# Gather of a deformable convolution: coefficients multiplied from PSUM, group outputs in one bank

## The reference

```python
def _L3_conv_ref(data_im, weight, offset_w, mask_w):
    ...
        w00 = ((1 - ly) * (1 - lx))[:, :, None]
        w01 = ((1 - ly) * lx)[:, :, None]
        w10 = (ly * (1 - lx))[:, :, None]
        w11 = (ly * lx)[:, :, None]
        val = w00 * gather(y0i, x0i) + w01 * gather(y0i, x1i) + w10 * gather(y1i, x0i) + w11 * gather(y1i, x1i)
        val = val * msk
        return val.reshape(B, C * K, Ho, Wo)
    offset = _conv(data_im, offset_w)
    mask = jax.nn.sigmoid(_conv(data_im, mask_w))
    col = _deform_im2col(data_im, offset, mask)
    out = jnp.einsum('op,bphw->bohw', weight, col)
    return out
...
x = x + _L0_conv_ref(_gn(x), L0_conv_mean_table, L0_conv_std_table, L0_conv_weight, L0_conv_bias, 4, 5, 5, 6)
x = x + _L1_conv_ref(_gn(x), L1_conv_gn_weight, L1_conv_gn_bias, L1_conv_w1, L1_conv_b1, L1_conv_w2, L1_conv_b2)
x = x + _L2_conv_ref(_gn(x), L2_conv_ln_w, L2_conv_ln_b, L2_conv_W_in, L2_conv_conv_w, L2_conv_conv_b, L2_conv_W_xproj, L2_conv_W_dt, L2_conv_b_dt, L2_conv_A_log, L2_conv_D, L2_conv_W_out)
x = x + _L3_conv_ref(_gn(x), L3_conv_weight, L3_conv_offset_w, L3_conv_mask_w)
```

## Time and profile before

| | us |
|---|---|
| median of three runs | 1004.47 (1001.02 to 1005.22) |
| the profiled execution | 999.45 |
| its span, first to last instruction | 997.5 |
| VectorE busy | 837.4 (84%) |
| TensorE busy | 780.8 (78%) |
| GpSimd busy | 574.7 (58%) |
| ScalarE busy | 375.1 (38%) |

### The profile page before, as it was taken

How to read it: one execution, slowest core, us unless ns; L and a number is a source line. 1 busy time by engine, 2 the same in 40 slices (tenths; PEclk the granted TensorE clock), 3 DMA queues, 4 the chain that set the end, 5 groups by cost and what they waited for, 6 DMA issues and landing times.

```text
span 997.5 us, 8280 instructions
## 1 busy us (share of the span) xinstructions
PE 780.8 (78%) x2364; PEld 372.8 (37%) x2365; DVE 837.4 (84%) x1164; ACT 375.1 (38%) x535; POOL 574.7 (58%) x528
## 2 busy tenths in 40 slices
PE   3445878587778688778777887768389999999996
PEld 1122323132322134444343544414265444444443
DVE  3888853899999778689999999985989989989994
ACT  1120056854445135311111111101067777686640
POOL 0000000177674047777777777777777777777774
PEclk9666989789999798567777777777569999999998
DMA  5000018000000541111111112137343735444422
GB/s 124 0 0 1 0 32 170 5 0 1 0 1 0 106 104 48 47 51 50 50 52 50 50 50 53 50 97 186 105 138 90 206 113 148 135 126 114 124 66 53
DMA packets 32339, 69.82 MB, mean 70 GB/s; under 512 B 12368, under 2 KB 12624, under 8 KB 31184
## 3 DMA queue, kind: packets, MB, share of 16 engines
q1 hardware_dynamic: 16080, 35.27, 13.1%
q0 software_dynamic: 15360, 31.49, 12.2%
q10 hardware_dynamic: 864, 2.64, 1.2%
HBM read 54.94 MB, written 5.77 MB: 61 GB/s over the span
## 4 chain that ended last, share of the span: by engine, by line
POOL 48%; issue 17%; DVE 11%; PE 7%; ACT 1%; DMA 1%; POOLq 0%; ACTq 0%; SPq 0%; DVEq 0%
POOL got L788 47%; DVE scratch L1185 6%; DVE scratch L1192 3%; PE PS L1064 1%; PE PS L922 1%; DMA G<-XN 1%; PE PS L1285 1%; PE PS L923 1%; PE PS L931 1%; PE PS L1057 1%; PE PS L941 1%; PE PS L1049 1%; ACT scratch L1143 0%; PE PS L624 0%; DVE st L138 0%
## 5 line engine op out<-in xcount | busy, mean ns | idle before, releaser
L788 POOL DMA_INDIRECT got<-corner_table,idx_slot x405 | 401.7, 992 | 123.4 <-issue 123.4
L1049 PE MATMUL PS<-parts,selb 96*128 96x512 bf16 (+1 forms) x256 | 89.3, 450 | 78.4 <-DVE scratch L1111 41.0
L1064 PE MATMUL PS<-scratch,wt 128*128 128x512 f32 x256 | 149.9, 717 | 0.5 <-DVE scratch L1192 0.5
L1492 PE MATMUL PS<-scratch,UZ 128*128 128x512 f32 (+1 forms) x288 | 133.6, 613 | 2.9 <-DVE scratch L1477 2.9
L788 POOL DMA_INDIRECT got<-corner_table,idx_all x75 | 80.6, 1075 | 60.7 <-DVE prime L1359 38.1
L823 PE MATMUL PS<-ln_g,w 128*128 128x32 f32 x576 | 97.2, 334 | 0.0
L823 PEld LDWEIGHTS PS<-ln_g,w 128*128 128x128 f32 x576 | 94.5, 257 | 0.0
L829 ACT ACTIVATE G<-PS 128x32 f32 (+1 forms) x32 | 6.2, 195 | 221.4 <-PE PS L823 221.3
L1064 PEld LDWEIGHTS PS<-scratch,wt 128*128 128x128 f32 x256 | 59.9, 234 | 59.4 <-issue 50.1
L1161 POOL TENSOR_TENSOR scratch<-scratch 128x1024 f32<-128x1024 f32 x16 | 37.6, 2348 | 77.1 <-ACT scratch L1143 77.1
L1469 ACT ACTIVATE scratch<-UZ,knot 128x512 f32<-128x512 f32 (+1 forms) x128 | 81.6, 708 | 0.4
(11 more groups left out here) (344 smaller groups left out, 1345.4 us busy)
## 6 DMA issues: line engine op xcount, KB each, us to landing
UZ<-dense_rows SPq DMA_DIRECT2D x24, 512.0 KB, 4.1
got<-corner_table,idx_slot POOLq DMA_INDIRECT x405, 2.5
UZ<-dense_rows SPq DMA_DIRECT2D x96, 64.0 KB, 2.2
XN<-ln_g SPq DMA_DIRECT2D x6, 256.0 KB, 5.1
got<-corner_table,idx_all POOLq DMA_INDIRECT x75, 2.6
corner_table<-scratch SPq DMA_DIRECT2D x1, 1056.0 KB
corner_table<-XN SPq DMA_DIRECT2D x1, 1056.0 KB
X<-in_x SPq DMA_DIRECT2D x4, 256.0 KB, 4.8
```

Of the source, the lines that this page charges most:

```text
L788: pool.indirect_dma_start(got[:, slot, tap, :, :].rearrange("p k c -> p (k c)"), None, tables[b], bass.IndirectOffsetOnAxis(ap=index[:, ta ...
L1049: last = nc.tensor.matmul(PS[:, first + n, :], selb[:, which, j, :], parts[:, bass.ds(i * CHUNK + n * BANK, BANK)], start=True, stop=True)
L1064: last = nc.tensor.matmul(PS[:, 4 + n, :], wt[:, W_SUM:W_SUM + P], dBC[:, j % 2, n * BANK:(n + 1) * BANK], start=False, stop=(j == PAIRS - 1))
L1492: last = nc.tensor.matmul(PS[:, n % 4, :], steps[rows, j, :, :].rearrange("p b c -> p (b c)"), ramps[k][rows, j, :], start=(j == 0), stop= ...
```

## The change

VectorE copies the coefficients of each group into bank 7, whose room is cut by slot, a group ahead, and the multiply reads them from there. The first copy stands at the end of `prepare(0)`, each further one between the multiply and the first addition of the turn before. The outputs of groups and pairs, which had banks 6 and 7 in turn, now share bank 6, in two parts of it; TensorE waits for the readout of the group (the pair) just before.

```diff
+        def coef_bank(slot, n=TAPS):
+            return PS[:, 7, slot * 4 * TAPS:slot * 4 * TAPS + 4 * n]
+
+        def next_coef(G, slot, n=TAPS):
+            return nc.vector.tensor_copy(coef_bank(slot, n), coef[:, bass.ds(G, 1), 0:n, :].rearrange("p o t k -> p (o t k)"))
...
             tell(v, nc.vector.tensor_tensor(prodg[:, 0:n, :, :].rearrange("p t k c -> p (t k) c"),
                                             got[:, slot, 0:n, :, :].rearrange("p t k c -> p (t k) c"),
-                                            coef[:, bass.ds(G, 1), 0:n, :].rearrange("p o t k -> p (o t k)").unsqueeze(2).to_broadcast([P, n * 4, C]),
+                                            coef_bank(slot, n).unsqueeze(2).to_broadcast([P, n * 4, C]),
                                             ALU.mult), l3["prod_done"], G + (SLOTS + 1))
+            next_coef(G + 1, (slot + 1) % SLOTS)
...
         def group_psum(slot):
-            return PS[:, 6 + slot % 2, 0:32]
+            return PS[:, 6, 32 * (slot % 2):32 * (slot % 2) + 32]
...
             pe.wait_ge(l3["col_done"], G + 1)
-            pe.wait_ge(l3["o_read"], G + (1 if slot else 2))
+            pe.wait_ge(l3["o_read"], G + 2)
...
         def pair_psum(m):
-            return PS[:, 6 + m % 2, 0:2 * C]
+            return PS[:, 6, 2 * C * (m % 2):2 * C * (m % 2 + 1)]
...
-                                            coef[:, G, 0:n, :].rearrange("p t k -> p (t k)").unsqueeze(2).to_broadcast([P, n * 4, C]),
+                                            coef_bank(slot, n).unsqueeze(2).to_broadcast([P, n * 4, C]),
                                             ALU.mult), l3["prod_done"], G + (SLOTS + 1))
+            if G + 1 < B * GROUPS:
+                next_coef(G + 1, (slot + 1) % SLOTS, n)
...
             pe.wait_ge(l3["col_done"], GROUPS + 2 * m + 2)
-            pe.wait_ge(l3["o_read"], max(33, 2 * m + 32))
+            pe.wait_ge(l3["o_read"], 2 * m + 34)
...
+                if b == 0:
+                    vchain(v, next_coef(0, 0))
                 between(2)
```

## The result

The changed kernel takes 1006.68 us (median of 20 runs, 1003.66 to 1010.96) against 1003.69 us of the kernel before in the same series (20 runs, 1000.65 to 1007.91): a ratio of 1.0033 with a 95% interval of 1.0023 to 1.0044, or +3.3 us (+2.3 to +4.4). The forecast was -0.3 us, with ends of -2.7 and +3.8. So the time is inside the range and within 0.5%, but on the other side of no change, and by more than the measurement is uncertain. The profiled execution of the changed kernel has a span of 1001.6 us (997.5 before); VectorE is busy for 843.2 us, TensorE for 780.4, GpSimd for 560.4.

The account below looks back on a forecast made before the run. The path was early gathers, VectorE's scan, TensorE's dense stream and a tail. Terms -2.7 (turn 4) + 2.8 + 0.3 (copies) + 0.55 (readout) - 1.29 (tail) = -0.3 us gave 1004.2 us; 8-in-10 range 996 to 1011 us.

Parts of the forecast that it names:

- The path: Whole kernel: gathers of groups 0 to 4, VectorE through batch 1's scan and preparation, TensorE's dense stream, a tail.
- The rival in which the gather's gain reaches the end: Dense stage: it follows VectorE, whose 17.2 us of gather waits go; about -10 us, 994 us; chance 0.11.
- The multiply from PSUM: VectorE's 64 multiplies: reading coefficients from PSUM in place of SBUF costs nothing.
- The slower repeated operand: VectorE's multiplies: PSUM values read 32 times cost more; at 0.35 us each, 8 us and 1012 us; chance 0.11.
- What it frees: First turns: gather issues no longer held by multiplies, so turn 4 begins 2.7 us earlier (ends 1.2 and 3.5).
- The copy: Behind the multiply: 0.14 us (ends 0.07, 0.25) in 20 loop turns, 2.8 us; 0.3 us in turns 25 to 27.
- The readout: Group 28, one output bank: TensorE waits for ScalarE to read out group 27, +0.55 us on the path.
- The tail: End of the kernel: VectorE's 1.29 us wait for the last group's gather goes, -1.29 us.
- another pattern of the granted clock: Ahead of the dense stretch: would move the time by a few us either way; no term in the sum.
- Putting the difference on the median: Forecast time: profiled execution lay 5 us under the timed runs' median, so -0.3 us was applied to 1004.47 us.

Follow-up runs that it names:

- the fixed address: Changed kernel, but the loop's copy behind the multiply always reads group 0's coefficients, so no register instruction precedes it; 1.0002 of the kernel before.
- Two copies: Changed kernel with a second copy of the same 36 coefficients right behind the first in the loop's 20 turns; 1.0084 of the kernel before.
- the lighter changed kernel: Changed kernel with one of nine slope products of each dense batch left out of TensorE's sum; 0.9897 of the kernel before.
- the version that pays only at both ends: Changed kernel with PSUM coefficients and copies only for groups 0 to 3 and 29 to 63, the others from SBUF; 0.9979 of the kernel before.

## Why the prediction was right or wrong

**The path** was right. TensorE's stream sets the pace of the dense stage: with one slope product less the changed kernel loses 13.6 us, while 10.6 us less of gathers bring nothing beyond, at most, the tail. The rival in which the gather's gain reaches the end falls with it.

**The multiply from PSUM** at nothing was right: 1346 ns in the mean against 1350 in the earlier trace rows. The slower repeated operand falls. The Trainium skill (VectorE: DVE Perf Modes, section on the TRN2 errata) tabulates 62 cycles more for a PSUM source than for an SBUF source; the trace doesn't show them in this instruction. **What it frees** was right in kind and size: 2.0 to 2.9 us at turn 4 in the two profiles, where 2.7 was taken. The page SBUF — State Buffer of the Trainium skill (Who interferes with whom) infers that an elementwise instruction with two tensors, as this multiply is, doesn't hold up descriptor generation; the two multiplies at 392 us, one with two SBUF inputs and an issue of 2.30 us beside it, one with a PSUM input and an issue of 0.94 us, are the same instruction in the same place and contradict it.

**The copy** is the step that failed. Its own price was right (0.11 us; 0.10 measured). The register instruction was counted at half its 57 ns, 0.03 us; behind the multiply's wait it costs 0.124 us, more than its own 75 ns, and nothing of it is hidden. The term is 20 x 0.227 = 4.5 us in place of 2.8. The upper end of the bound (0.25 us) covers that number by luck: it was taken for a copy whose 0.2 us are wholly exposed, not for the register instruction. The trace of the kernel before already showed the price, in the one loop turn where the register instruction has no cover because VectorE has just waited for a gather. In turn 4 it begins at 422.3 us, behind the index copy at 422.22 us, and the multiply follows that copy by 0.23 us, where in the other 19 turns it follows by 0.08 us at most:

```profile
422.45 1.36 DVE L799 TENSOR_TENSOR prodg<-got,coef 128x1152 f32<-128x1152 f32 x1
```

**The readout** at group 28 was right: TensorE waits 0.44 us there for ScalarE (0.55 taken), and in the kernel before the shared bank alone changes nothing that can be measured. **The tail** is the second term that failed: the 1.29 us were read from one execution and counted as certain, while the kernel before in its second profile, and with the shared bank alone, has no wait there to give up. The term is between 0 and -1.29.

The sum with measured terms: -2.4 (turn 4, middle of two profiles) + 4.5 + 0.3 + 0.44 - 1.29 = +1.5 us, or +2.8 us where the tail gives nothing. The copy's term alone turns the sign. Against the measured 3.3 us (2.3 to 4.4), 1.8 us are missing by the first sum and 0.5 us by the second, and 0.5 lies inside the interval: the terms may be all there is, or leave up to some 3 us open.

With the same terms the fixed address comes to -1.4 (its own turn 4) + 2.1 + 0.3 + 0.44 = +1.4 us, or +0.2 with the tail; measured is +0.2 (-1.3 to 1.8), so nothing is missing. Two copies come to -2.1 + 4.5 + 2.0 + 0.3 + 0.44 = +5.1, or +3.9 with the tail; measured is 8.4 (6.6 to 10.2), so 3.3 or 4.5 us are missing. The waits of VectorE for TensorE in the scan are 7.5 us in the profile of the fixed address, 7.2 in that of the changed kernel and 11.2 in that of two copies. That a later turn brings more of these waits is a possible cause, which the prediction had only as another pattern of the granted clock worth "a few us either way", with no term in its sum. It is not shown: the kernel before has 5.6 us of them in one profile and 11.5 in the other, the lighter changed kernel, whose scan is that of the changed one, has 12.3, and no run here holds the clock while the scan's length changes.

Putting the difference on the median was sound, but the profile of before was a favourable one: its scan was the shortest of all that were taken, so it showed few of the scan's waits for TensorE, and a wait at the end that another execution doesn't have.

## What to carry to other kernels

Look at where an added instruction's address is worked out: a register instruction that was free under a running instruction costs more than its own length where the engine has nothing to run (0.124 us for one of 75 ns behind a wait here), and in a loop it is paid each time; issue the instruction ahead of the wait, or give it a fixed address. Relieve an engine only where somebody waits for it: here the first four groups held nearly all of the gain (the tail had 1.29 us at most), and paying for relief in the 20 turns between lost it, while the version that pays only at both ends is 2.1 us faster than before (0.1 to 4.1). When two engines end within a microsecond or two of each other, ten microseconds taken from one alone bring one at most. Which of the two ends last, and by how much, can change from one execution to the next: read the end of more than one profile before pricing it.

## What the runs showed that was not expected

A register instruction of 57 to 82 ns behind a wait moved the next instruction by 0.124 us. A small copy of 0.20 us costs its successor 0.10 us, alone or as the second of two. The scan of one kernel took 227.4 us in one execution and 233.7 in another, by waits of about 1 us that appear where a group's 18 matmuls meet the granted clock at 0.50 (4.03 us) rather than 1.00 (2.17 us). And 2.0 us of instructions added to that scan cost 5.1 us in the time, of which the rest is not explained. The chain of work that ended last was GpSimd's for 48% of the span in one execution of the kernel before and for 5% in another.
